# Output products of the older tile ahead of the w1 products of the newer one in TensorE's step of an expert stage

## Chip, cores and metric

The kernel runs on one core of a Trainium2 chip. The metric is the device time of one execution in microseconds (us), the median of several runs. The kernel is written by hand: each engine has its own instruction stream, and semaphores that the program names order the engines against each other.

## What is computed

A graph layer stack (two layers over 128 samples of 128 rows of 384) is followed by a mixture of experts over all 16384 rows, each of which goes to one of eight experts. The change lies in the expert stage, which computes this (`x` is what the graph layers left, cut to what matters):

```python
routes = jnp.argmax(route_prob, axis=-1)
onehot = jax.nn.one_hot(routes, E, dtype=xt.dtype)
h = jnp.einsum('td,edr->ter', xt, w1) + b1[None]
h = jax.nn.gelu(h, approximate=False)
h = h * onehot[..., None]
out = jnp.einsum('ter,erd->td', h, w2) + onehot @ b2
out = out * route_prob_max[:, None]
x = x + out
```

`xt` is the layer-normalised `x`, 384 wide; `w1` takes it to 64, `w2` back to 384.

## The kernel before

**The first stage**, about nine tenths of the time, is the graph layers with the routing worked in. It writes every row, with its scale, shift, route probability and number, to a bucket of its expert in DRAM. The change does not touch it.

**The expert stage** reads the buckets in 72 tiles of 256 rows (`TILES`; a tile is T = 2 halves of 128 rows), all rows of a tile with one expert. What happens to a tile j:

- SyncE loads it into `tok` (a ring of eight).
- ScalarE (L1477) normalises half 0 and VectorE (L1526) half 1 into `n2_rows` (shown as n_rows).
- TensorE, `turn` (L1430): six 128x128 transposes into `turn_banks`.
- ScalarE copies two thirds of the result out (L1496), VectorE the last third (L1533), into `n2T`. ScalarE also picks the expert's w1 and bias (L1486, L1490).
- TensorE, `hidden` (L1442): three fp32 products with w1, which the trace shows as six matmuls of 256 columns, into one of two `hidden_banks`.
- ScalarE, `gelu` (L1505).
- VectorE, `gelu_high` (L1539) and `gelu_low` (L1543): the gelu's value as two fp32r parts, in a ring of four (`GELUS`).
- TensorE, `output` (L1455, L1456): for each half t two products with w2 into `y_banks[t]`. There is one bank for each half and no second one: the products of tile j's half t wait until VectorE has read tile j-1's (`pe.wait_ge(y_ready, ...)`, L1453).
- VectorE, `combine` (L1552): for each half, bank times route probability plus the row, into `out_rows`; this is what raises `y_ready`.
- GpSimd (L1592): two indirect DMAs scatter the rows into the output.

Every engine walks through steps i = 0, 1, 2, ... (a loop of eight steps a turn, L1380, with the first and the last steps written out), and each engine has its own `step(i, k)`, in which the order of the work is written by hand. TensorE works in step i on `turn(i-1)`, `hidden(i-2)` and `output(i-4)`; ScalarE on `normalise(i)`, `pick_w1(i-1)`, `copy_first(i-1)`, `gelu(i-2)`. VectorE's is this, with DEPTH = 5:

```python
if there(i - DEPTH):
    combine(i - DEPTH, (k - DEPTH) % RING)
if there(i):
    normalise(i, k)
if there(i - 1):
    copy_last(i - 1, k - 1)
if there(i - 2):
    gelu_high(i - 2, k - 2)
    gelu_low(i - 2, k - 2)
```

Each engine takes its instructions in the order written; one that waits holds all behind it on its engine.

Of the kernel before, what the change touches and what calls it, by code (L numbers as in the profile page):

```python
# [25 lines left out]
def build(nc, x, adj, Wl, bl, Ws, bs, Wr, br, ln_w, ln_b,  # L26
# [14 lines left out]
    RING = 8  # L41
# [5 lines left out]
    with ctx:  # L47
# [1296 lines left out]
        with ffn_ctx:  # L1344
# [29 lines left out]
            OUTPUT, GELUS, DEPTH = 4, 4, 5  # L1374

            def tiles(eng, step):

                for i in range(RING):
                    step(i, i)
                with eng.Fori(1, TILES // RING) as block_of:  # L1380
                    for k in range(RING):
                        step(block_of * RING + k, k)
                for i in range(TILES, TILES + DEPTH):
                    step(i, i % RING)

            def there(j):
                return not isinstance(j, int) or 0 <= j < TILES

            def past(j, n):

                return not isinstance(j, int) or j >= n

            with nc.Block() as block:  # L1393
# [24 lines left out]
                @block.tensor  # L1418
                def _(pe):
                    def turn(j, k):  # L1420
                        pe.wait_ge(n2_act_ready, j + 1)
                        pe.wait_ge(n2_dve_ready, j + 1)
                        if past(j, 2):
                            pe.wait_ge(first_copied, j - 1)
                            pe.wait_ge(last_copied, j - 1)
                        first, last_bank = turn_banks[k % 2]
                        for c in range(C):
                            o = first[:, c * TILE:(c + 1) * TILE] if c < 2 else last_bank[:, 0:TILE]
                            for t in range(T):
                                last = pe.transpose(o[:, t * P:(t + 1) * P],  # L1430
                                                    n2_rows[k % 2][:, t, c * P:(c + 1) * P], ident[:])
                        last.then_inc(turned, 1)

                    def hidden(j, k):
                        pe.wait_ge(w1_picked, j + 1)
                        pe.wait_ge(first_copied, j + 1)
                        pe.wait_ge(last_copied, j + 1)
                        if past(j, 2):
                            pe.wait_ge(gelu_ready, j - 1)
                        o = hidden_banks[k % 2][:, 0:TILE]  # L1440
                        for c in range(C):
                            last = pe.matmul(o, w1_pick[k % 2][:, c, :, :].rearrange("p h r -> p (h r)"),  # L1442
                                             n2T[k % 2][:, c, :], start=(c == 0), stop=(c == C - 1))
                        last.then_inc(hidden_done, 1)

                    def output(j, k):
                        e = pe.value_load(tile_expert[0:1, j:j + 1] if isinstance(j, int) else
                                          tile_expert[0:1, bass.ds(j, 1)], min_val=0, max_val=E - 1)
                        pe.wait_ge(gelu_top_ready, j + 1)
                        pe.wait_ge(gelu_bottom_ready, j + 1)  # L1450
                        for t in range(T):
                            if past(j, 1):
                                pe.wait_ge(y_ready, T * (j - 1) + t + 1)  # L1453
                            o, rows = y_banks[t][:, 0:D], slice(t * P, (t + 1) * P)
                            pe.matmul(o, gelu_top[k % GELUS][:, rows], w2_top[:, e, :], start=True, stop=False)  # L1455
                            pe.matmul(o, gelu_bottom[k % GELUS][:, rows], w2_bottom[:, e, :], start=False, stop=True  # L1456
                                      ).then_inc(y_done, 1)

                    def step(i, k):
                        if there(i - 1):  # L1460
                            turn(i - 1, k - 1)
                        if there(i - 2):
                            hidden(i - 2, k - 2)
                        if there(i - OUTPUT):
                            output(i - OUTPUT, (k - OUTPUT) % RING)

                    pe.wait_ge(tiles_ready, 2)
                    pe.wait_ge(ones_set, 3 * GELUS)
                    tiles(pe, step)

                @block.scalar
# [164 lines left out]
```

## Time and profile before

| | |
|---|---|
| median of 3 runs | 2161.67 us (2161.18 to 2163.12) |
| the profiled execution's own time | 2160.51 us |
| its span in the profile | 2158.7 us |
| TensorE (PE), share of the span busy | 97% |
| VectorE (DVE) | 77% |
| ScalarE (ACT) | 69% |
| GpSimd (POOL) | 65% |
| first transposes of the expert stage | at 1948.5 us |

PE is TensorE's matmuls and PEld its weight loads, which run beside them. A timeline row gives the start and the time taken, both in us, the engine, the line of the program, the operation, the tile written and those read, the shape where it is known, and how many instructions of a kind were merged; in brackets the idle time of the engine before it and who ended it ("issue": nothing that the profile shows). A row of merged instructions runs from the first one's start to the last one's end. A matmul's time contains the pipeline's depth, so that matmuls in a row start closer together than their times are long. Columns of an answer by stretches: the stretch, its length, then busy us (and instructions) of PE, PEld, DVE, ACT and POOL, the granted TensorE clock as a share of 2.4 GHz, the share of the DMA engines busy, and GB/s.

### The profile page before, as it was taken

Reading aid. Unit: us, or ns where it says so; the run is one execution under the profiler, and the core shown is the slowest. Engines: PE = TensorE matmul, PEld = TensorE weight load, DVE = VectorE, ACT = ScalarE, POOL = GpSimd, SP = SyncE. Lnnn points to the kernel's source line nnn. Section 1 sums busy time; section 2 is a strip of 40 time slices with the busy share of each in tenths; the row PEclk is TensorE's granted clock in tenths of the full one; section 3 lists DMA queues with packets and bytes.
Section 4 is the critical chain, followed back from the end, with each engine's and each line's share of the span. In section 5 each row is a group of like instructions: output and inputs, shape, how many; then the busy total and the mean of one; then the engine's idle time right before and its main releaser. Section 6 shows DMA issues by size and latency. Waiting matters only on the chain. (4 is left out here: it accounts for less than half of the span.)

```text
span 2158.7 us, 56998 instructions
## 1 busy us (share of the span) xinstructions
PE 2091.0 (97%) x13580; PEld 2038.0 (94%) x13581; DVE 1656.5 (77%) x5452; ACT 1491.7 (69%) x3901; POOL 1413.0 (65%) x3348
## 2 busy tenths in 40 slices
PE   6999999999999999999999999999999999968997
PEld 5999999999999999999999999999999999957996
DVE  5777777777777777677777777777777777758997
ACT  4777767667776776676776776677776767637775
POOL 2556666666666666666666666666666666655887
PEclk9999999999999999999999999999999999978999
DMA  7101111211111111111111111111111111117995
GB/s 194 32 27 50 38 49 48 104 50 47 43 49 50 51 42 50 43 47 47 43 46 50 47 42 50 44 50 50 50 39 50 47 39 49 34 56 234 279 294 192
DMA packets 94261, 153.77 MB, mean 71 GB/s; under 512 B 17621, under 2 KB 70619, under 8 KB 93954
## 3 DMA queue, kind: packets, MB, share of 16 engines
q1 hardware_dynamic: 75844, 99.61, 16.0%
q0 software_dynamic: 17408, 50.62, 6.1%
q8 instruction: 114, 1.87, 0.4%
q14 instruction: 191, 1.56, 0.3%
q10 hardware_dynamic: 704, 0.10, 0.0%
HBM read 96.11 MB, written 57.32 MB: 71 GB/s over the span
## 5 line engine op out<-in xcount | busy, mean ns | idle before, releaser
L422 PE MATMUL bank<-wT_hi,hT_hi 128*128 128x384 f32 x2304 | 798.8, 347 | 11.3 <-issue 4.8
L424 PE MATMUL bank<-wT_hi,hT_lo 128*128 128x384 f32 x2304 | 774.2, 336 | 0.0
L423 PE MATMUL bank<-wT_lo,hT_hi 128*128 128x384 f32 x2304 | 773.1, 336 | 0.0
L422 PEld LDWEIGHTS bank<-wT_hi,hT_hi 128*128 128x128 f32 x2304 | 434.9, 189 | 20.5 <-ACT bank L622 12.4
L423 PEld LDWEIGHTS bank<-wT_lo,hT_hi 128*128 128x128 f32 x2304 | 435.2, 189 | 0.0
L424 PEld LDWEIGHTS bank<-wT_hi,hT_lo 128*128 128x128 f32 x2304 | 434.0, 188 | 0.0
L1173 POOL TENSOR_TENSOR hT_lo<-hT,hT_hi 128x384 fp32r<-128x384 f32 x256 | 261.5, 1022 | 22.9 <-ACT hT_hi L687 21.3
L682 ACT ACTIVATE hT<-bank 128x384 f32<-128x384 f32 x256 | 125.9, 492 | 203.0 <-PE bank L414 183.5
L658 ACT CAST right_hi<-bank 128x384 fp32r<-128x384 f32 x256 | 122.6, 479 | 173.9 <-PE bank L424 173.2
L1228 POOL TENSOR_SCALAR_AFFINE_SELECT deltaT_hi<-turned_hi 128x128 fp32r<-128x128 f32 x256 | 85.3, 333 | 211.8 <-ACT turned_hi L664 209.2
L414 PE MATMUL bank<-hT 128*128 128x128 f32 x1536 | 213.3, 275 | 0.0
L813 DVE CUSTOM_DVE_ANT_0 delta<-bank,adj_in 128x128 f32<-128x128 f32 x256 | 74.7, 292 | 173.2 <-ACT bank L615 152.6
L414 PEld LDWEIGHTS bank<-hT 128*128 128x128 f32 x1536 | 191.6, 192 | 0.0
L1236 POOL TENSOR_SCALAR_AFFINE_SELECT deltaT_lo<-turned_lo 128x128 fp32r<-128x128 f32 x256 | 74.9, 293 | 157.1 <-DVE turned_lo L870 156.7
L1592 POOL DMA_INDIRECT out_dram<-out_rows,row_ids x144 | 144.4, 1003 | 42.9 <-issue 22.8
L1217 POOL DMA_INDIRECT buckets<-rows,dest_words x128 | 138.8, 1084 | 31.9 <-issue 24.6
L838 DVE SCALAR_TENSOR_TENSOR bank<-bank,mv,gamma 128x384 f32<-128x384 f32 x256 | 158.0, 617 | 0.2 <-issue 0.2
L640 ACT ACTIVATE bank<-bank,sum_own 128x384 f32<-128x384 f32 x256 | 141.7, 554 | 21.2 <-DVE sum_own L816 20.0
L1258 POOL TENSOR_TENSOR out_scale<-var_e,minus_half 128x1 f32<-128x1 f32 x256 | 140.5, 549 | 20.6 <-POOL var_e L1253 1.1
L654 ACT CAST left_hi<-bank 128x384 fp32r<-128x384 f32 x256 | 122.0, 477 | 46.0 <-PE bank L424 44.2
L828 DVE BATCH_NORM_STATS2 bn<-bank 128x6 f32<-128x384 f32 x256 | 143.1, 559 | 6.8 <-PE bank L465 5.9
L858 DVE TENSOR_TENSOR left_lo<-bank,left_hi 128x384 fp32r<-128x384 f32 x256 | 140.2, 548 | 10.1 <-ACT left_hi L654 9.1
(201 smaller groups left out, 5145.2 us busy)
## 6 DMA issues: line engine op xcount, KB each, us to landing
tok<-buckets SPq DMA_DIRECT2D x72, 388.0 KB, 4.5
x_in<-in_x_dram SPq DMA_DIRECT2D x128, 192.0 KB, 2.5
x_res<-in_x_dram SPq DMA_DIRECT2D x128, 192.0 KB, 2.4
adj_in<-in_adj_dram SPq DMA_DIRECT2D x128, 64.0 KB, 2.4
buckets<-pads SPq DMA_DIRECT2D x9, 388.0 KB, 4.9
out_dram<-out_rows,row_ids POOLq DMA_INDIRECT x144
buckets<-rows,dest_words POOLq DMA_INDIRECT x128, 2.7
w_top<-in_L_ffn_w_dram SPq DMA_DIRECT2D x2, 768.0 KB
```

The source lines that it names most:

```text
L414: last = pe.matmul(score_bank[:, SCORES], hc, hc, start=(c == 0), stop=(c == C - 1))
L422: pe.matmul(o, hi, w_hi, start=False, stop=False, skip_group_check=True)
L423: pe.matmul(o, hi, w_lo, start=False, stop=False, skip_group_check=True)
L424: last = pe.matmul(o, lo, w_hi, start=False, stop=(c == C - 1), skip_group_check=True)
L640: act.activation(ctx_banks[odd][:, 0:D], self_bank[:, 0:D], ACT.Copy, scale=sum_own[odd][:, 0:1]).then_inc(selfterm_ready, 1)
L828: dve.bn_stats(bn[odd][:], ctx_banks[odd][:, 0:D]).then_inc(bn_done, 1)
L838: dve.scalar_tensor_tensor(o, o, mv[odd][:, 0:1], gamma[:, w[1], :], ALU.subtract, ALU.mult).then_inc(centred, 1)
L858: dve.tensor_tensor(left_lo[:], left_bank[:, 0:D], left_hi[:].bitcast(F32), ALU.subtract).then_inc(leftlo_ready, 1)
L1173: pool.tensor_tensor(hT_lo[odd][:], hT[:], hT_hi[odd][:].bitcast(F32), ALU.subtract).then_inc(hTlo_ready, 1)
L1217: pool.indirect_dma_start(buckets, bass.IndirectOffsetOnAxis(ap=dest_words[:, slot:slot + 1].bitcast(U32), axis=0), rows[:, slot, :], None ...
L1258: pool.tensor_tensor(out_scale[odd][:], var_e[odd][:], minus_half[:, 0:1], ALU.pow).then_inc(scale_ready, 1)
L1592: pool.indirect_dma_start(out.rearrange("b s d -> (b s) d"), bass.IndirectOffsetOnAxis(ap=row_ids[k][:, t:t + 1].bitcast(U32), axis=0), ou ...
```

## The change

In TensorE's step, `output(i-4)` is written ahead of `hidden(i-2)` instead of behind it. Nothing else differs, and every wait keeps its condition.

```diff
                     def step(i, k):
                         if there(i - 1):
                             turn(i - 1, k - 1)
+                        if there(i - OUTPUT):
+                            output(i - OUTPUT, (k - OUTPUT) % RING)
                         if there(i - 2):
                             hidden(i - 2, k - 2)
-                        if there(i - OUTPUT):
-                            output(i - OUTPUT, (k - OUTPUT) % RING)
```

TensorE's instructions in one step of the loop before, with the semaphores each waits for (L1430 transposes, L1442 w1 products, L1447 the load of the expert's number into a register, L1455 and L1456 output products; ISA and REGISTER_ALU are the sequencer's own):

```order
L1430 MATMUL bank<-ident,n_rows 128x128 [waits first_copied,last_copied,n2_dve_ready,n2_act_ready]
L1430 MATMUL bank<-ident,n_rows 128x128 x5
L1442 MATMUL bank<-n2T,w_pick 128x256 [waits last_copied,gelu_ready,first_copied,w1_picked]
L1442 MATMUL bank<-n2T,w_pick 128x256 x2
L1447 TENSOR_LOAD tile_expert
L1447 ISA x2
L1455 ISA [waits y_ready,gelu_bottom_ready,gelu_top_ready]
L1455 MATMUL bank<-w_top,gelu_top 128x384
L1456 REGISTER_ALU
L1456 MATMUL bank<-w_bottom,gelu_bottom 128x384
L1455 MATMUL bank<-w_top,gelu_top 128x384 [waits y_ready]
L1456 MATMUL bank<-w_bottom,gelu_bottom 128x384
```

The same step of the changed kernel:

```order
L1430 MATMUL bank<-ident,n_rows 128x128 [waits first_copied,last_copied,n2_dve_ready,n2_act_ready]
L1430 MATMUL bank<-ident,n_rows 128x128 x5
L1447 TENSOR_LOAD tile_expert
L1447 ISA x2
L1455 ISA [waits y_ready,gelu_bottom_ready,gelu_top_ready]
L1455 MATMUL bank<-w_top,gelu_top 128x384
L1456 REGISTER_ALU
L1456 MATMUL bank<-w_bottom,gelu_bottom 128x384
L1455 MATMUL bank<-w_top,gelu_top 128x384 [waits y_ready]
L1456 MATMUL bank<-w_bottom,gelu_bottom 128x384
L1442 MATMUL bank<-n2T,w_pick 128x256 [waits last_copied,gelu_ready,first_copied,w1_picked]
L1442 MATMUL bank<-n2T,w_pick 128x256 x2
```

The w1 products now stand behind both waits on `y_ready`. VectorE's order, which raises `y_ready` at L1552, is the same in both kernels:

```order
L1552 SCALAR_TENSOR_TENSOR out_rows<-bank,tok 128x384 [waits stored1,y_done]
L1549 REGISTER_ALU
L1552 SCALAR_TENSOR_TENSOR out_rows<-bank,tok 128x384 [waits y_done]
L1526 TENSOR_SCALAR n_rows<-tok 128x384 [waits turned,tok_loaded2]
L1530 REGISTER_ALU
L1533 COPY n2T<-bank 128x256 [waits hidden_done,turned]
L1539 CAST gelu_top<-gelu_out 128x256 [waits y_done,gelu_ready]
L1543 TENSOR_TENSOR gelu_bottom<-gelu_out,gelu_top 64x256 [waits gelu_top_ready]
```

Here too nothing moved: the pair of combines stands right behind the last step's L1543.

## Rows read from the trace of the kernel before

**Rows 1.** Busy time by stretches, middle of the expert stage.
```profile
2000.00:2040.00 40.00, 40.00 (x240) 36.16 (x240) 37.25 (x91) 31.14 (x75) 32.88 (x46) 1.00 0.89 274
```
**Rows 2.** Groups of instructions, 1960 to 2130 us, the expert stage.
```profile
L1442 PE MATMUL bank<-n2T,w_pick 128*128 128x256 f32 x384 | 93.5, 380 | 0.0
...
L1505 ACT ACTIVATE gelu_out<-bank,b_pick 128x256 f32<-128x256 f32 x64 | 30.4, 475 | 31.7 <-PE bank L1442 30.5 <-issue 1.1
```
**Rows 3.** Timeline of one step, TensorE, ScalarE and VectorE.
```profile
2036.71 0.75 PEld L1430 LDWEIGHTS bank<-ident,n_rows 128*128 128x128 f32 x6
...
2037.42 1.17 PEld L1442 LDWEIGHTS bank<-n2T,w_pick 128*128 128x128 f32 x6
2037.53 1.46 PE L1442 MATMUL bank<-n2T,w_pick 128*128 128x256 f32 x6
2037.56 1.13 DVE L1552 SCALAR_TENSOR_TENSOR out_rows<-bank,tok 128x384 f32<-128x384 f32 x2
...
2038.62 0.19 PEld L1455 LDWEIGHTS bank<-w_top,gelu_top 128*128 128x128 f32 x1
...
2039.03 0.47 ACT L1505 ACTIVATE gelu_out<-bank,b_pick 128x256 f32<-128x256 f32 x1 [0.60 <-PE bank L1442]
2039.18 0.34 PE L1455 MATMUL bank<-w_top,gelu_top 128*128 x1
...
2039.35 0.34 PE L1456 MATMUL bank<-w_bottom,gelu_bottom 128*128 x1
...
2039.36 0.75 PEld L1430 LDWEIGHTS bank<-ident,n_rows 128*128 128x128 f32 x6
...
2039.54 0.29 DVE L1539 CAST gelu_top<-gelu_out 128x256 fp32r<-128x256 f32 x1
...
2039.87 0.42 DVE L1543 TENSOR_TENSOR gelu_bottom<-gelu_out,gelu_top 64x256 fp32r<-64x256 f32 x1
...
2040.21 1.13 DVE L1552 SCALAR_TENSOR_TENSOR out_rows<-bank,tok 128x384 f32<-128x384 f32 x2
```
**Rows 4.** Timeline of a step in which the output products were held by y_ready.
```profile
2032.45 1.14 DVE L1552 SCALAR_TENSOR_TENSOR out_rows<-bank,tok 128x384 f32<-128x384 f32 x2 [0.35 <-issue]
...
2033.20 0.19 PEld L1455 LDWEIGHTS bank<-w_top,gelu_top 128*128 128x128 f32 x1
...
2033.64 0.19 PEld L1455 LDWEIGHTS bank<-w_top,gelu_top 128*128 128x128 f32 x1
...
2033.93 0.34 PE L1456 MATMUL bank<-w_bottom,gelu_bottom 128*128 x1
```
**Rows 5.** Idle before the combines (L1552), 1960 to 2130 us: who, us, times.
```profile
  issue: 2.8, 8
```
**Rows 6.** Timeline: w1 products of tiles 2 and 71, outputs of tile 0.
```profile
1956.91 1.17 PEld L1442 LDWEIGHTS bank<-n2T,w_pick 128*128 128x128 f32 x6
...
1958.10 0.19 PEld L1455 LDWEIGHTS bank<-w_top,gelu_top 128*128 128x128 f32 x1
...
1958.84 0.75 PEld L1430 LDWEIGHTS bank<-ident,n_rows 128*128 128x128 f32 x6
...
2140.90 1.23 PEld L1442 LDWEIGHTS bank<-n2T,w_pick 128*128 128x128 f32 x6
```
**Rows 7.** TensorE's clock after gaps: by stretches, then timeline.
```profile
1900.00:1915.00 15.00, 12.08 (x81) 11.24 (x78) 10.73 (x39) 8.47 (x24) 7.42 (x18) 1.00 0.12 41
...
1920.00:1925.00 5.00, 3.24 (x16) 2.39 (x16) 2.90 (x10) 0.87 (x4) 2.57 (x6) 0.54 0.01 3
```
**Rows 8.** TensorE's timeline around such gaps, and cold w1 products.
```profile
1910.59 0.44 PE L422 MATMUL bank<-wT_hi,hT_hi 128*128 128x384 f32 x1 [1.19 <-ACT bank L622]
...
1920.42 0.60 PE L517 MATMUL bank<-one_hot,earlier 128*128 128x32 f32 x2 [2.65 <-issue]
...
1951.59 2.88 PE L1442 MATMUL bank<-n2T,w_pick 128*128 128x256 f32 x6
```
**Rows 9.** The sequencer's load of the expert's number (L1447), 1960 to 2130 us.
```profile
L1447 PEldq TENSOR_LOAD <-tile_expert x63: 297/325/838, 1961.8 to 2128.1; - x63
```

## The prediction

> **What bounds the kernel now.** I read the busy times by stretches first. In the expert stage TensorE is busy without a break, at the full clock, while VectorE has 37.25 us of work in 40 [rows 1]. The groups for 1960 to 2130 us show nothing idle before TensorE's w1 products, and ScalarE waiting for them, 30.5 us in all over 64 tiles [rows 2]. So before the change TensorE's own work sets the pace of this stage. The timeline of one step gives its size: transposes to transposes 2039.36 - 2036.71 = 2.65 us [rows 3]. Over the whole stage, from the w1 products of tile 2 to those of tile 71, it is (2140.90 - 1956.91) / 69 = 2.667 us a tile [rows 6].
>
> The reader should then see in that timeline how near the output products are to their wait. Tile j's products need both halves of `combine(j-1)` to be over. The combines began at 2037.56 and took 1.13 us, to 2038.69. The first output product loads its weights at 2038.62, a little before the second half's combine ends, and the second half's at about 2039.0: each is met with a few tenths to spare [rows 3]. In the order of the change the same products are due straight after the transposes, at 2037.42, where the combine has not begun.
>
> **The change part by part.** Nothing is added or removed: each tile has the same six transposes, six w1 matmuls and four output matmuls, and no DMA and no other engine's instruction moves. What changes is which work is held behind which wait.
>
> *The wait.* In VectorE's step the combine of tile i-5 stands behind `gelu_low` of the step before, that is of tile i-3. That one comes from `hidden(i-3)`, which TensorE does in step i-1. In the old order `hidden(i-2)` of step i ran while this was going on, ahead of the wait. In the new one it stands behind `output(i-4)`, which needs `combine(i-5)`. So the w1 products of one step now wait for a chain that began with the w1 products of the step before, and a step can't be shorter than this chain:
>
> - End of the second half's combine to the start of its output products' weight load, where they were held: 2032.45 + 1.14 = 2033.59, to 2033.64, 0.05 us [rows 4].
> - From there to the second output matmul, 2033.93 - 2033.64 = 0.29 us [rows 4], and from it to the first w1 matmul one spacing of such matmuls, 2039.35 - 2039.18 = 0.17 us [rows 3].
> - First w1 matmul to the gelu that waits for the last one: 2039.03 - 2037.53 = 1.50 us [rows 3].
> - Gelu to `gelu_high`: 2039.54 - 2039.03 = 0.51; `gelu_high` to `gelu_low`: 2039.87 - 2039.54 = 0.33; `gelu_low` to the first combine: 2040.21 - 2039.87 = 0.34 us [rows 3].
> - Both combines, 1.13 us [rows 3].
>
> The sum is 0.05 + 0.29 + 0.17 + 1.50 + 0.51 + 0.33 + 0.34 + 1.13 = 4.32 us, against 2.667 now. The first half's output products are not in it: released at about 2033.05, they load at 2033.20 and are through when the second half's combine ends [rows 4].
>
> *The ends of the loop of eight steps.* VectorE sat idle before a combine 8 times for "issue", 2.8 us in all, 0.35 each [rows 5], and the row of such a step shows it just before the combine [rows 4]. Before, TensorE mostly worked over it. Now it lies in the chain: +2.8 us. TensorE's own branch falls into its wait: nothing.
>
> *The first step.* `output(0)` now stands ahead of `hidden(2)`. Four output matmuls take 1958.84 - 1958.10 = 0.74 us [rows 6], and tile 0's gelu is long done: +0.74 us, once. From step 5 on the chain rules, 69 times, up to the w1 products of tile 71.
>
> *What lies beside.* The transposes follow the w1 products and need 0.75 us of the 0.51 + 0.33 + 0.34 + 1.13 us that the chain then spends elsewhere. ScalarE's and VectorE's other work (VectorE has 37.25 us in 40 now [rows 1], so some 2.5 a step) falls into steps of 4.3 us. The load of the expert's number, 0.33 us and rarely more [rows 9], is issued after the transposes, inside the wait. Loads and stores get more time for the same bytes. The end is as before: the last gelu, its combines and its stores follow the w1 products of tile 71 in both orders, so what tile 71's products are late the kernel is late.
>
> *The sum.* 0.74 + 69 x (4.32 - 2.667) + 2.8 = 0.74 + 114.1 + 2.8 = 117.6 us. The profiled execution took 2160.51 us with a span of 2158.7; the median of the runs is 1.2 us above that execution, so the sum goes onto the median: 2161.7 + 117.6 = **2279 us**.
>
> *The bounds.* A hold ahead of fp32 w1 products doesn't occur in the trace. From below, TensorE refills as if it had not been held: two spacings of 0.17 in place of 0.51 [rows 3], 0.17 less a step, 2268 us. From above, the w1 products' own waits are looked at one after another behind the released product. The nearest row is the first half's release, 0.15 us from 2033.05 to 2033.20 [rows 4]; twice that is 0.3 a step, 2300 us. I take the rows of the held step as they are, since that is the same wait on the same instruction.
>
> *The clock.* The new wait leaves TensorE idle in every step: from the end of the transposes, 2.1 us after the first w1 matmul (their weight loads begin 2038.62 - 2037.53 = 1.09 after it and take 0.75 [rows 3], and the last matmul ends some 0.2 later), to the first half's output products at 1.50 + 0.51 + 0.33 + 0.34 + 0.60 + 0.15 = 3.4, so 1.3 us. Near rows: between 1900 and 1915 us it was idle for 1.19 us ahead of a product and the granted clock was 1.00 over the stretch; at 1920.42 it had been idle for 2.65 us and the clock of the next stretch was 0.54 [rows 7, 8]. 1.3 is nearer to 1.19, so the sum has the clock at 2.4 GHz. The Trainium skill speaks against this change here: "TensorE: Matmul & The Clock Gate", section "A second HAM failure mode: psum-queue depth-cycling", says that small idle times between groups of matmuls, from going round the PSUM banks, made the clock go to and fro between its two levels. By it the time would be that of the first rival; the trace shows no stretch that idles so in every step.
>
> **The rivals.**
>
> *The clock falls to 1.2 GHz in part of the steps.* At that level the w1 products took 2.88 us for 1.46 [rows 8, 3], +1.42 in the chain, and doubling the two spacings of 0.17 adds 0.3: +1.7 us a step. In all 69 steps +119, 2398 us; in half of them 2339. For it: 1.3 us of idleness 70 times in a row, and a stage that begins at the low clock. Against it: the row at 1910 us, and at the low clock TensorE has more to do in each step, which lifts its busy share again.
>
> *The load of the expert's number lies in the chain.* If the sequencer comes to it only when the combine is over, the longest one, 0.84 us [rows 9], adds up to 58 us: 2337 us. Against it: nothing holds the sequencer between the transposes and this load.
>
> *Not slower: the output products find their bank free.* This is how it reads from TensorE alone: products of an older tile, with gelus long done, go ahead of those that need fresh copies. The place is the wait for y_ready (L1453), the price is zero while the chain fits into 2.65 us, and it then gives 2162 us; it may take back some of the longer steps such as that of rows 4, 1 us or so. It decides from a chain of under 2.65 us, and the three VectorE terms and the w1 products alone are 1.50 + 0.33 + 0.34 + 1.13 = 3.3. It needs a link to be missing: that VectorE's combine did not have to follow `gelu_low`. VectorE works in the written order, and the rows show the combine 0.34 us behind it.
>
> **How the numbers follow.** The forecast, the chain at the full clock, gets 0.86; the falling clock 0.09, the register load 0.03, the free bank 0.02. The range is 2267 to 2300 us: the bounds of the hold. The two slower rivals lie above it and stay out, with the missing link below it, 0.14 together. No change, for a measurement of this kernel, is about 0.2% (4.3 us): faster 0.01, within it 0.01, slower 0.98.
>
> **What would show it.** The step of the changed kernel: transposes to transposes 4.3 to 4.4 us; the first half's output products starting about 0.13 us behind the end of the first combine, the second half's 0.05 behind the second; an idle time of about 1.3 us before L1455, where none was, put down to the combine; the chain that ended last passing VectorE's and ScalarE's lines in every step and no longer TensorE's alone; TensorE's busy share in the stage down to about 70%, ScalarE and VectorE idle by 1.5 us a step more than now; the granted clock at 1.00; and the first nine tenths of the span unchanged. The forecast is wrong if the steps stay under 3.5 us (a link is not in the chain), if the w1 products take 2.9 us (the clock), or if the second output product starts late behind its combine (a cost of the release that rows 4 don't have).

## The result and the profile after

The changed kernel takes **2283.18 us** (median of 4, 2282.08 to 2283.70), the kernel before beside it 2162.15: ratio 1.0561 (95% interval 1.0547 to 1.0574), 121.0 us more. The forecast was 2279, range 2267 to 2300.

From the page of the changed kernel: its span, the busy shares (97, 77, 69 and 65% in the table of the kernel before), and TensorE's busy share and clock in 40 slices of 57 us.

```profile
span 2281.7 us, 57006 instructions
PE 2118.1 (93%) x13580; PEld 2039.1 (89%) x13581; DVE 1656.2 (73%) x5452; ACT 1495.3 (66%) x3901; POOL 1414.1 (62%) x3348
PE   6999999999999999999999999999999996667665
PEclk9999999999999999999999999999999998899998
```

The busy times of VectorE, ScalarE and GpSimd are within 4 us of what they were (DVE 1656.2 us, 1656.5 before), so their shares fell with the longer span. TensorE's reads 2118.1 us for 2091.0 with the same 13580 matmuls: a group that is held no longer overlaps the tail of the one before it. The change shows in the last slices alone. The busy times by stretches, as in [rows 1]:

```profile
2040.00:2080.00 40.00, 27.51 (x149) 22.19 (x148) 22.46 (x54) 19.19 (x45) 20.20 (x28) 1.00 0.57 166
2080.00:2120.00 40.00, 27.73 (x142) 22.14 (x140) 22.55 (x54) 19.63 (x45) 19.25 (x27) 0.96 0.59 177
```

TensorE is down from 40.00 to 27.5 in 40 us, VectorE from 37.25 to 22.5, ScalarE from 31.1 to 19.2: no engine's own work is the bound any more. The second stretch has a clock of 0.96.

One step of the changed kernel, timeline, in the order of [rows 3] (half of the rows left out):

```profile
2101.64 1.23 PEld L1442 LDWEIGHTS bank<-n2T,w_pick 128*128 128x128 f32 x6
2101.82 1.46 PE L1442 MATMUL bank<-n2T,w_pick 128*128 128x256 f32 x6
...
2102.90 0.79 PEld L1430 LDWEIGHTS bank<-ident,n_rows 128*128 128x128 f32 x6
...
2103.31 0.47 ACT L1505 ACTIVATE gelu_out<-bank,b_pick 128x256 f32<-128x256 f32 x1 [1.97 <-PE bank L1442]
...
2103.82 0.29 DVE L1539 CAST gelu_top<-gelu_out 128x256 fp32r<-128x256 f32 x1 [1.79 <-ACT gelu_out L1505]
...
2104.14 0.42 DVE L1543 TENSOR_TENSOR gelu_bottom<-gelu_out,gelu_top 64x256 fp32r<-64x256 f32 x1
2104.49 1.13 DVE L1552 SCALAR_TENSOR_TENSOR out_rows<-bank,tok 128x384 f32<-128x384 f32 x2
...
2105.23 0.19 PEld L1455 LDWEIGHTS bank<-w_top,gelu_top 128*128 128x128 f32 x1 [1.54 <-issue]
2105.24 0.44 PE L1455 MATMUL bank<-w_top,gelu_top 128*128 x1 [1.31 <-DVE out_rows L1552]
...
2105.67 0.19 PEld L1455 LDWEIGHTS bank<-w_top,gelu_top 128*128 128x128 f32 x1
...
2105.95 1.23 PEld L1442 LDWEIGHTS bank<-n2T,w_pick 128*128 128x128 f32 x6
2106.12 1.46 PE L1442 MATMUL bank<-n2T,w_pick 128*128 128x256 f32 x6
```

Read it downwards as one chain, which TensorE, ScalarE and VectorE pass to each other: w1 products, gelu, its two parts, both combines, output products, w1 products, each starting when the one above lets it. From 2101.64 to 2105.95 are 4.31 us. TensorE idles 1.31 us, put down to the combine. Who waited for whom, 1965 to 2250 us, some 65 steps (us in all, times, the longest):

```profile
ACT gelu_out L1505 <- PE bank L1442: 140.1, 65, 3.7
DVE gelu_top L1539 <- ACT gelu_out L1505: 121.3, 65, 3.2
...
PE bank L1455 <- DVE out_rows L1552: 87.9, 64, 1.8
```

ScalarE waits for TensorE, VectorE for ScalarE and TensorE for VectorE, every one in every step, a full circle. Before, the first of the three was there [rows 2]; from 1960 to 2130 us the second came once, for 0.4 us, and the third not at all.

### The profile page after: what moved, and what is told of

Same layout as the page of the kernel before. It is cut to its first block and busy times, and to the rows that moved or that the text cites. A ratio compares the mean times of both kernels' runs of the same rounds, so it can differ in the third digit from the quotient of the medians.

```text
span 2281.7 us, 57006 instructions
## 1 busy us (share of the span) xinstructions
PE 2118.1 (93%) x13580; PEld 2039.1 (89%) x13581; DVE 1656.2 (73%) x5452; ACT 1495.3 (66%) x3901; POOL 1414.1 (62%) x3348
## 5 line engine op out<-in xcount | busy, mean ns | idle before, releaser
L1217 POOL DMA_INDIRECT buckets<-rows,dest_words x128 | 138.9, 1085 | 31.1 <-issue 24.9
L1455 PE MATMUL bank<-w_top,gelu_top 128*128 x144 | 62.4, 433 | 98.5 <-DVE out_rows L1552 98.2
```

Of the source, the lines that this page charges most:

```text
L1217: pool.indirect_dma_start(buckets, bass.IndirectOffsetOnAxis(ap=dest_words[:, slot:slot + 1].bitcast(U32), axis=0), rows[:, slot, :], None ...
```

## The experiments

The kernel before was run beside each. One step is counted from the first w1 weight load of a tile to that of the next; a mean step is over the 69 from tile 2 to tile 71. The diffs below are cut short: `if there(...)` and its call stand on one line, and arguments are left out (`...`). VectorE's full order is quoted in the section on the kernel before.

**Open one link (e1).** The first kernel keeps the changed order of TensorE and moves VectorE's combine:

```diff
-OUTPUT, GELUS, DEPTH = 4, 4, 5
+OUTPUT, GELUS, DEPTH = 4, 4, 4
-if there(i - DEPTH): combine(i - DEPTH, ...)
 if there(i): normalise(i, k)
 if there(i - 1): copy_last(i - 1, k - 1)
+if there(i - DEPTH): combine(i - DEPTH, ...)
 if there(i - 2): gelu_high(...); gelu_low(...)
```

> TensorE's order as in the changed kernel; VectorE's combine moves behind copy_last and ahead of gelu_high, one tile newer (DEPTH 4). The chain theory: output(i-4) waits for combine(i-5), which VectorE has now done a step before gelu_high(i-3) let it go on, so no w1 product is in the loop any more and TensorE's own 2.65 us sets the step again: 2162 us, between 2159 and 2165, no idle time of TensorE before L1455. The rival that the new order itself costs the time, because TensorE has to work with one bank for each half and gets to it too early after the last use: the bank and TensorE's order are as in the changed kernel, so the step stays at 4.3 us and the time near 2283.

Measured: 2166.46 us against 2162.13, ratio 1.0018 (1.0009 to 1.0027). With VectorE's pair of combines moved, and taken one tile sooner (as are GpSimd's stores, which go by the same DEPTH), 117 of the 121 us are gone, while TensorE's order and its single bank for each half are those of the changed kernel. The rival falls. The last 4 us were not expected. The mean step is 2.748 us, only 33 of the 69 under 2.68 and none over 3.35. TensorE's weight loads show idle time in such steps:

```profile
2036.89 0.79 PEld L1430 LDWEIGHTS bank<-ident,n_rows 128*128 128x128 f32 x6
2037.90 0.19 PEld L1455 LDWEIGHTS bank<-w_top,gelu_top 128*128 128x128 f32 x1 [0.21 <-issue]
```

It is an idle time for "issue" between the transposes and the output products, 21 times from 1965 to 2145 us, 5.3 us in all. That is the place of the register load (L1447). It took this long from 1965 to 2145 us (least, median, most, in ns):

```profile
L1447 PEldq TENSOR_LOAD <-tile_expert x65: 298/497/722, 1967.5 to 2143.9; - x65
```

In the old order the w1 products, whose weight loads take 1.2 us, cover it; in the new one only 0.65 us of transposes do.

**The same chain over two steps (e2).** The changed kernel with its output products one step later:

```diff
-OUTPUT, GELUS, DEPTH = 4, 4, 5
+OUTPUT, GELUS, DEPTH = 5, 4, 5
```

> The changed kernel with output(i-5) in the place of output(i-4) (OUTPUT 5), all else alike. The chain theory: the combine of tile i-5 in VectorE's step i is followed by output(i-4) in TensorE's step i+1, so the same eight links, 4.32 us, now span two steps, 2.16 each, under the 2.65 of TensorE's own work: 2162 us, between 2159 and 2167. The rival that the w1 products suffer from standing behind any output products: the step stays at 4.3 us, 2283.

Measured: 2216.31 us, ratio 1.0251 (1.0235 to 1.0266), mean step 3.478: better than the changed kernel by 67 us and a miss by 54. The first chain is gone from the trace, and another has come:

```profile
2042.16 1.15 DVE L1552 SCALAR_TENSOR_TENSOR out_rows<-bank,tok 128x384 f32<-128x384 f32 x2 [0.33 <-PE bank L1456]
...
2043.22 0.47 DVE L1526 TENSOR_SCALAR n_rows<-tok 128x384 f32<-128x384 f32 x1
...
2043.76 0.64 PEld L1430 LDWEIGHTS bank<-ident,n_rows 128*128 128x128 f32 x6 [0.40 <-issue]
...
2044.86 0.19 PEld L1455 LDWEIGHTS bank<-w_top,gelu_top 128*128 128x128 f32 x1 [0.46 <-issue]
...
2045.61 1.14 DVE L1552 SCALAR_TENSOR_TENSOR out_rows<-bank,tok 128x384 f32<-128x384 f32 x2 [0.41 <-PE bank L1456]
```

The combine now needs the output products of its own step, `normalise` stands behind it, the next transposes need `normalise`, and the output products stand behind those: 1.06 + 0.54 + 1.10 + 0.75 = 3.45 us. The expectation had followed only the chain that it opened.

**Two more links (e3).** The changed kernel with the combine (still of tile i-5) behind `normalise` and `copy_last`:

```diff
-if there(i - DEPTH): combine(i - DEPTH, ...)
 if there(i): normalise(i, k)
 if there(i - 1): copy_last(i - 1, k - 1)
+if there(i - DEPTH): combine(i - DEPTH, ...)
```

> The changed kernel with VectorE's combine(i-5) moved behind normalise(i) and copy_last(i-1), still a step after the gelu_low it follows. The chain theory: two more VectorE instructions in every turn of the loop, 0.38 us each from start to start, so a step of 4.32 + 0.77 = 5.09 and 2283 + 69 x 0.77 = 2336 us. If VectorE's place in the chain were not what counts (it idles 1.8 us a step, which would hold both instructions): 2283.

Measured: 2403.52 us, ratio 1.1112 (1.1095 to 1.1129). Slower, as the chain theory says and no other, but by 120 us where it says 53. The steps tell why: four take 5.03 or 5.04 us (4.32 + 0.72, against 5.09 forecast), most between 6.1 and 7.0. By stretches, this kernel:

```profile
2000.00:2120.00 120.00, 84.18 (x304) 67.32 (x304) 45.71 (x111) 38.56 (x92) 41.74 (x57) 0.76 0.40 118
```

**The same with TensorE kept busy (e10).** To part the chain from the clock, e3 with each tile's transposes done twice, which changes no value:

```diff
-for c in range(C):
+for c in [*range(C), *range(C)]:
     o = first[:, c * TILE:(c + 1) * TILE] if c < 2 else last_bank[:, 0:TILE]
```

> The third experiment (two more VectorE links in the chain) came to 2404 us where the chain at the full clock gives 2336; its granted clock was 0.77 in the stage and its steps alternated between 5.04 us and about 6.5. Here every tile's transposes are done twice on top of it, 0.65 us more work for TensorE inside its idle time. If the 68 us were the clock, which TensorE loses by idling 2.3 us a step, and the added work keeps it: steps of 5.05, 2283 + 69 x 0.73 = 2333 us, less 3 for the falls that the changed kernel has itself, so some 2330: a kernel that does more and is 70 us faster. If the chain is longer than I count: 2404 or more.

Measured: 2329.43 us (2328.33 to 2332.70), 74 us less than e3, though TensorE has 72 x 0.65 = 47 us more of work. The same stretch:

```profile
2000.00:2120.00 120.00, 86.52 (x513) 72.78 (x512) 57.41 (x138) 49.72 (x116) 51.52 (x70) 0.99 0.50 145
```

The granted clock is 0.99 for 0.76 and the median step 5.03. So of e3's 120 us the two links are 46 (2329.4 - 2283.2) to 50 us (69 x 0.72), and the clock the other 70 to 74. (This run was on another chip; see below. Its steps, over 3.6 us, are not touched by what is told there.)

**Half of the order (e4).** Only the first half's output products go ahead of the w1 products (the register load is then done twice, once for each half):

```diff
 turn(i - 1, k - 1)
+output(i - OUTPUT, ..., [0])   # first half
 hidden(i - 2, k - 2)
+output(i - OUTPUT, ..., [1])   # second half
```

> Only the first half's output products stand ahead of the w1 products, the second half's behind them. The chain theory: the second combine's 0.53 us and its 0.05 of release leave the chain, the first half's slower release (0.14) comes in: 1.50 + 0.51 + 0.33 + 0.34 + 0.60 + 0.14 + 0.29 + 0.17 = 3.88 us a step against 4.32, 2283 - 69 x 0.44 = 2253 us. The rival that the wait costs a fixed amount however it is placed: 2283. The rival that half the order brings half the loss: 2222.

Measured: 2252.08 us (2250.66 to 2253.09), ratio 1.0419 (1.0403 to 1.0435), median step 3.88: 1 us from the forecast; both rivals fall. The row that carries it: the w1 products start behind the first combine only (here the combine's line is 1554).

```profile
2104.65 1.13 DVE L1554 SCALAR_TENSOR_TENSOR out_rows<-bank,tok 128x384 f32<-128x384 f32 x2
...
2105.39 0.19 PEld L1455 LDWEIGHTS bank<-w_top,gelu_top 128*128 128x128 f32 x1 [1.48 <-issue]
...
2105.72 1.19 PEld L1442 LDWEIGHTS bank<-n2T,w_pick 128*128 128x128 f32 x6
```

**More work for TensorE, in both orders (e5, e6).** The transposes twice, in the changed kernel and in the kernel before:

> The changed kernel with every tile's six transposes done twice (same inputs, same bank). The chain theory: TensorE idles 1.4 us ahead of each held output product and the second six take 0.65 us there, so the step stays at 4.32; the busier TensorE should also not lose its clock any more (it fell three times in the middle of the stage and once near its end, some 1 us each): 2280 us, between 2278 and 2284. A theory in which TensorE's amount of work still counts expects 2283 + 72 x 0.65 = 2330.

> The kernel before with the transposes done twice, beside the same edit on the changed kernel. If TensorE's own work bounds the old order, as the forecast has it, all of it shows: 2162 + 72 x 0.65 = 2209 us. If VectorE (2.5 us of work in a step of 2.65) or the transfers (0.9 of the DMA engines' time) are as near a bound as TensorE, the loss is about the same, since they have no more to do; if TensorE had slack, it is less, down to 2162.

Measured: 2281.30 us for e5 (2279.87 to 2282.67) and 2204.00 for e6 (ratio 1.0188, 1.0172 to 1.0204). The same 0.65 us a tile cost 41 us in the old order and nothing in the new one. By stretches, first e5:

```profile
2000.00:2120.00 120.00, 99.81 (x602) 84.06 (x601) 67.45 (x162) 58.19 (x136) 60.36 (x83) 1.00 0.58 171
```

then e6:

```profile
2000.00:2120.00 120.00, 120.00 (x800) 113.06 (x799) 91.20 (x219) 78.77 (x182) 94.00 (x109) 1.00 0.78 234
```

TensorE bounds the old order and has room in the new. In e6 every step but the last, which has no transposes, is 3.30 to 3.32 us, those at the ends of the loop of eight too. In the kernel before those ends show as longer steps, 2.0 us together. That is part of the 5 us by which 2209 was too much; the stretch from tile 2 to tile 71 also holds the added work of only 68 of the 72 tiles. In e5 the w1 products took longer than 1.46 us at the last tile alone, and its mean step is 4.397 us against 4.447, 3.5 us over the stage; the two medians are 1.9 us apart, within the spread of the runs.

**The old order with the combine moved (e7).** e1's whole edit, on the kernel before.

> The kernel before (w1 products first) with VectorE's combine(i-4) ahead of gelu_high, as in the first experiment. The chain theory: TensorE's 2.65 us bound the step either way: 2162, between 2160 and 2165, and the order of the change is then neutral by itself. If the gelus' parts come late now, since gelu_high waits for the combine of products that end a step: 2170 or more.

Measured: 2162.11 us against 2162.89, ratio 0.9996 (0.9987 to 1.0005): the same. 63 of 69 steps are under 2.68 us, 56 in the kernel before; it is not a gain that the times can show.

**The register load (e11, e8, e12).** First the changed kernel with the load of the expert's number ahead of `turn` (e11), then e1 with the same edit (e8, and again as e12):

```diff
+e = expert(i - OUTPUT)          # the register load alone
 turn(i - 1, k - 1)
-output(i - OUTPUT, ...)
+output(i - OUTPUT, ..., e)
```

> The changed kernel with only the register load moved ahead of the transposes. In the changed kernel the load falls into the wait for the combine, except in the first step with output products, where TensorE idled 0.5 us: 2282 us, between 2280 and 2285. If the load were in the chain of every step (the prediction's second rival): up to 58 us less, 2225.

Measured: 2282.76 us (2278.61 to 2283.76), with the median step still 4.31 us: the load is not in the chain.

> The first experiment (combine ahead of gelu_high) came to 2166, with steps between 2.65 and 3.2 us; its trace shows the sequencer's load of the expert's number taking up to 0.7 us between the transposes and the output products. Here that load stands ahead of the transposes, so that the older w1 products cover it. If the load was what those steps waited for: every step 2.65 us and 2161 us, between 2158 and 2163; the end of the kernel was 1.7 us shorter in the changed order, which may bring it to 2159, just under the kernel before. If something else made them long (VectorE with 2.5 us of work in a step, the stores): 2166 again.

Measured: 2223.81 us, and beside it the kernel before took 2223.42 (2218.83 to 2229.94): ratio 0.9995 (0.9985 to 1.0005). These four, e8 to e11, ran on another chip, on which the expert stage's transfers are slower. In e8's middle stretch the last number, GB/s, is 212, where the kernel before had 288 over the same stretch:

```profile
2000.00:2120.00 120.00, 98.36 (x533) 84.23 (x534) 85.92 (x201) 70.45 (x169) 79.63 (x100) 0.96 0.69 212
```

e8's mean step is 3.63 us there. 35 of its 69 steps are under 2.68 us, but 28 are over 3.35, among them 4 to 6 us long ones, and 9.0 once. Kernels whose steps are longer than that mean (e10, e11) took what they should.

> The same kernel as e8_load_ahead_of_turn, once more. There the kernel before, run beside it, took 2223 us instead of 2162, and the transfers of the expert stage moved 212 GB/s where they moved 288: both kernels were held by their loads, so that run says nothing on the register load. If the transfers are again at 280 GB/s or more: steps of 2.65 us without the 2.8 to 3.2 of the first experiment, 2161 us, between 2158 and 2163, against 2166 if the register load was not what made those steps long. If they are at 212 GB/s again: 2223, equal to the kernel before, and the question stays open.

Measured: 2219.24 us against 2216.90, ratio 1.0009 (0.9999 to 1.0019), 214 GB/s. So whether the load is the whole of e1's 4 us stays open. What speaks for it: of the steps not over 3.35 us, e8 has 35 of 41 under 2.68 and e12 34 of 39, e1 33 of 69.

**The loop of e2 opened (e9).** e2 with `normalise` ahead of `combine` in VectorE's step:

```diff
-if there(i - DEPTH): combine(i - DEPTH, ...)
 if there(i): normalise(i, k)
+if there(i - DEPTH): combine(i - DEPTH, ...)
 if there(i - 1): copy_last(i - 1, k - 1)
```

> The second experiment (output(i-5)) came to 2216 us, where the chain theory said 2162. Its trace shows another loop of 3.45 us: combine(i-5) to normalise(i) 1.06, to the transposes 0.54, to the output products of the next step 1.10 (the register load lies in it), to their combine 0.75. Here VectorE's normalise(i) goes ahead of combine(i-5), which opens that loop and leaves the first chain spread over two steps. If that loop is all there was: 2166 us, as in the first experiment, between 2160 and 2172. If the output products' place ahead of the w1 products costs by itself: 2216 or more.

Measured, on the same slower chip: 2225.19 us against 2223.42, ratio 1.0000 (0.999 to 1.001). There it can't be told from the kernel before, so the output products' place costs nothing that shows beside the transfers; the 2166 that were expected were not tested. 32 of its 69 steps are under 3.35 us, 8 of e2's.

## Why the prediction was right

**The bound.** Right, that TensorE's 2.65 us set the step before (e6: its added work shows almost in full) and that it would not afterwards (e5: it doesn't show at all). GpSimd was close behind, as told under "The end".

**The wait, 4.32 us a step.** Right in each term. In the step shown: w1 products to gelu 1.49 us (1.50 forecast), gelu to `gelu_high` 0.51 (0.51), to `gelu_low` 0.32 (0.33), to the combine 0.35 (0.34), both combines 1.13 (1.13), release 0.05 (0.05), second output product to the w1 products' first matmul 6.12 - 5.67 = 0.45 (0.46). Sum 4.30, the step's 4.31 but for rounding. The first half's release was 0.14 us, and TensorE's busy share 69%. That the second combine and VectorE's order are links is shown by e4, e3 and e1, which shorten, lengthen and open the chain, by 0.43, 0.72 and all of it. What the experiments do not try is a second bank for each half; that the single bank couples the steps rests on the code and the wait's row.

**The ends of the loop of eight.** Right mechanism, 2.5 us too small (5.3 for 2.8). Between the w1 products of tile 2 and tile 71, at 1958.72 and 2265.58, lie 306.9 us:

```profile
1958.72 1.23 PEld L1442 LDWEIGHTS bank<-n2T,w_pick 128*128 128x128 f32 x6
...
2265.58 2.36 PEld L1442 LDWEIGHTS bank<-n2T,w_pick 128*128 128x128 f32 x6
```

69 x 4.32 are 298.1. e5, which does not lose its clock, has 303.4 there, so the loop's ends cost 5.3 us: a pair of steps of about 4.76 and 4.56 us in each turn. In the first of the two, `gelu_low` to the combine takes 0.76 us for 0.34, which is VectorE's branch: it was counted, at 0.35. In the second, the gelu starts 1.63 us behind the first w1 matmul for 1.50, and `gelu_high` 0.62 behind the gelu for 0.51: ScalarE's end of the loop and what VectorE adds there were not counted.

**The clock.** The forecast took 1.3 us of idleness as harmless and gave the rival, a falling clock, 9 in 100. The clock fell three times in the middle of the stage, and again towards tile 71. One of the three:

```profile
2082.41 0.44 PE L1455 MATMUL bank<-w_top,gelu_top 128*128 x1 [1.74 <-DVE out_rows L1552]
...
2083.30 2.48 PE L1442 MATMUL bank<-n2T,w_pick 128*128 128x256 f32 x6
```

against 1.46 at the full clock ([rows 8] have 2.88, all of it at the low one). Together 306.9 - 303.4 = 3.5 us, which the sum lacks. The row above it shows where: at an end of the loop of eight, where TensorE had been idle for 1.74 us. The other two (w1 products at 2011.77 and 2154.67) stand at such ends too, after 1.78 and 1.74 us, and the last w1 products (2.45 us) after 2.06. The w1 products of the ordinary steps, 50 of them after 1.31 to 1.41 us of idleness, took 1.46 us at most. So 1.3 us was harmless here, as the forecast had it; what it did not ask was how long TensorE idles at the ends of the loop. Three of the eight ends cost the clock, so the length of the idle time alone does not decide it. The sentence of the Trainium skill ("TensorE: Matmul & The Clock Gate", section "A second HAM failure mode: psum-queue depth-cycling") describes small idle times between groups, and a clock that goes to and fro. The trace agrees for the longer of its idle times; in e3, with TensorE idle 2.03 us ahead of its output products instead of 1.31, the clock falls in most steps.

**The first step.** 0.74 us forecast, 0.96 measured (tile 0's w1 products to tile 2's, 6.33 us for 5.37). The stage itself began 0.85 us later in this execution, which is not the change's.

**The end.** Forecast as before, measured 2281.7 - 2265.6 = 16.1 us from tile 71's w1 products to the end of the span, for 17.8, though tile 71's w1 products took 1.0 us longer at the low clock. The kernel ends with GpSimd's scatters, one every 1.29 us; 7 of them start behind tile 71's w1 products here, 11 in the kernel before. Two of the four are the order's: tile 69's output products are now done by then (e6, in the old order but with steps of 3.30 us, has 9). With the other two GpSimd was behind: a tile's pair of scatters took it 2.67 us there against a step of 2.65, and from a first combine's end to its scatter it was 0.9 us at tile 0 and 3.1 at tile 67. In the changed kernel this stays at 0.85. The forecast took the end as the same in both orders. The account: 0.96 + (306.9 - 184.0) + 0.85 - 1.7 = 123.0 us, the difference of the two spans (the medians of the runs differ by 121.0).

**The range.** It was drawn for the hold alone, and the hold came as the rows had it. The miss of 4 us is made of terms that the range was not made for: 2.5 us at the ends of the loop and 3.5 of clock too little, 1.7 at the end too much; the first step adds 0.2.

**The rivals.** The register load is not in the chain (e11), though it is 0.5 us in the first step with output products (5.81 us from tile 0 to tile 2 in e11 for 6.33), and it may be what e1 lacks, which is not shown. "Not slower" needed VectorE's combine to be free of `gelu_low`; e1 gives it just that, and 2166 us.

## What to carry to other kernels

Where two engines walk in steps by hand-written orders, write down the circle: from one instruction in a step, through every wait and everything that stands ahead on the same engine, back to that instruction one step later. The step is at least the circle's length divided by the steps it spans; here, moving old work that had long been ready ahead of fresh work put the fresh work behind a wait, and the release of that wait hung on fresh work of another engine. Ask for the length of the longest step too, not only of the usual one: the loop's ends cost here twice what was counted, and the clock fell there. After opening one circle, look for the next longest before trusting the new time (e2).

## What the runs showed of the hardware

- In the changed kernel, e10 and e11 every fall of TensorE's granted clock in the middle of the stage came at an end of the loop, after 1.74 to 1.81 us of idleness: three, one and two of the eight ends, with w1 products of 2.2 to 2.8 us for 1.46. After the 1.31 us (1.37 in e10) of the usual steps none fell. That is not a limit: in e8 w1 products took 2.76 us after two idle times in one step, of 1.01 and 1.39 us. With 2.03 us idle in the usual step (e3) the clock was 0.76 of full over 120 us, and about 70 us of a 120 us loss were that. Repeating the transposes, with no other use, shortened the idle time to 1.37 us and won the time back (2403.5 to 2329.4 us).
- GpSimd's pair of scatters for a tile took 2.67 us (1.30 and 1.37 from start to start in the kernel before), just over the step of 2.65: by tile 67 it had fallen 2 us behind, which showed at the end of the kernel. In steps of 3.30 us (e6) and 4.31 it did not. So in the kernel before GpSimd was all but a second bound.
- A register load from memory in TensorE's sequencer took 0.30 to 0.72 us in e1; with only 0.65 us of transposes to cover it and what follows it, TensorE stood still for 0.2 us, as in the rows of e1.
- The same kernel before took 2162 us on some chips and 2217 to 2223 on others, with 212 to 214 GB/s in the expert stage (e8, e12) in place of 288. There the changed order with its load moved (e11) is at 1.026 (1.0241 to 1.0278) of the kernel before, half of the loss elsewhere: e11's own time is the same, while the kernel before is held by something else already. What makes those chips slower was not found.
